# Row-shifted copies for three depthwise convolutions: sixteen on-chip transfers of 32 partitions in place of a DRAM round trip, and a shorter lag of one convolution

## The reference, cut to what matters

```python
t = t + dwconv(t, cpe1_w, cpe1_b)             # "cpe1"
tn = layernorm(t)
act_res = silu(tn @ actproj_w + actproj_b)
ti = silu(dwconv(tn @ inproj_w + inproj_b, dwc_w, dwc_b))      # "dwc"
out = linear_attention(ti) + dwconv(ti, lepe_w, lepe_b)        # "lepe"
t = shortcut + (out * act_res) @ outproj_w + outproj_b
```

## Time and profile before

| what | value |
|---|---|
| median of the runs shown (lowest, highest) | 3899.55 us (3897.82, 3903.65) |
| the profiled execution's own time | 3894.08 us |
| its span, first to last instruction | 3892.3 us |
| PE busy | 2998.4 us, 77% |
| DVE busy | 2489.5 us, 64% |
| ACT busy | 2366.1 us, 61% |
| POOL busy | 1088.2 us, 28% |
| mean granted TensorE clock | 0.92 of full speed |
| loads of shifted rows | 3 x 192 transfers of 196 KB, 3.8 to 3.9 us from issue to landing |
| stores to the scratch tensors | 3 x 48 transfers of 392 or 490 KB |

### The profile page before, as it was taken

One profiled execution on the slowest core, in us unless ns is written; L12 is line 12 of the kernel. 1 busy time (PEld: TensorE's weight loads), 2 busy tenths in 40 slices (PEclk: granted clock), 3 DMA queues, 4 the chain that ended last, 5 costly groups with the idle time before them and its releaser, 6 DMA issues. The chain is left out here.

```text
span 3892.3 us, 53786 instructions
## 1 busy us (share of the span) xinstructions
PE 2998.4 (77%) x17500; PEld 1615.2 (41%) x17500; DVE 2489.5 (64%) x2565; ACT 2366.1 (61%) x2681; POOL 1088.2 (28%) x612
## 2 busy tenths in 40 slices
PE   3678766969968876697996877677898778768699
PEld 2344334435534432543553433343454334344355
DVE  5677546876568644787466964578735886466871
ACT  3788434458778743546777864443767876444485
POOL 0235002632034500363103530046210452014530
PEclk9899988989989998898998999888999999988899
DMA  2001454600200146350020024644002004455201
GB/s 67 12 1 33 117 136 147 164 9 0 74 17 0 38 118 191 107 144 9 0 90 1 0 74 110 188 119 107 9 9 81 0 0 112 110 167 143 67 0 49
DMA packets 137194, 274.36 MB, mean 70 GB/s; under 512 B 17139, under 2 KB 93622, under 8 KB 137014
## 3 DMA queue, kind: packets, MB, share of 16 engines
q1 hardware_dynamic: 137014, 272.01, 25.3%
HBM read 194.07 MB, written 77.88 MB: 70 GB/s over the span
## 5 line engine op out<-in xcount | busy, mean ns | idle before, releaser
L1472 DVE SCALAR_TENSOR_TENSOR work<-region,cols,work 128x768 f32<-128x768 f32 x288 | 392.1, 1361 | 15.1 <-DVE work L1472 7.5
L664 POOL TENSOR_TENSOR region<-region 128x768 f32<-128x768 f32 x96 | 211.0, 2201 | 370.8 <-ACT region L844 365.1
L995 PE MATMUL psum<-region,m_fc 128*128 128x384 f32 (+1 forms) x768 | 282.2, 490 | 11.2 <-ACT work L946 11.2
L1241 PE MATMUL psum<-work,m_fc 128*128 128x384 f32 x768 | 282.6, 491 | 0.0
L995 PE MATMUL psum<-region,m_cen 128*128 128x384 f32 (+1 forms) x384 | 165.6, 557 | 136.5 <-DVE region L1585 62.3
L625 POOL TENSOR_TENSOR work<-work 128x768 f32<-128x768 f32 x48 | 113.9, 2377 | 501.8 <-ACT work L764 415.2
L1391 DVE SCALAR_TENSOR_TENSOR work<-region,cols,work 128x768 f32<-128x768 f32 x144 | 202.3, 1430 | 78.3 <-POOL work L625 62.3
L639 POOL TENSOR_TENSOR work<-work,region 128x768 f32<-128x768 f32 x96 | 174.3, 1816 | 235.0 <-DVE work L1406 235.0
L995 PE MATMUL psum<-work,m_avg 128*128 128x384 f32 x576 | 225.5, 516 | 15.6 <-ACT work L806 7.7
L217 DVE SCALAR_TENSOR_TENSOR region<-region,cols 128x768 f32<-128x768 f32 x192 | 223.8, 1166 | 16.7 <-POOL region L664 8.7
L678 POOL COPY region<-work 128x768 f32<-128x768 f32 x4 | 3.3, 823 | 818.6 <-DVE work L1509 818.6
(11 more groups left out here) (234 smaller groups left out, 7495.6 us busy)
## 6 DMA issues: line engine op xcount, KB each, us to landing
work<-scratch_cpe SPq DMA_DIRECT2D x192, 196.0 KB, 3.8
work<-scratch_dwc SPq DMA_DIRECT2D x192, 196.0 KB, 3.8
work<-scratch_lepe SPq DMA_DIRECT2D x192, 196.0 KB, 3.9
region<-in_tab_ch SPq DMA_DIRECT2D x48, 768.0 KB, 5.3
region<-in_x SPq DMA_DIRECT2D x48, 384.0 KB, 3.3
region<-in_tab_tok SPq DMA_DIRECT2D x48, 384.0 KB, 3.1
out<-work SPq DMA_DIRECT2D x48, 384.0 KB, 2.3
scratch_cpe<-region SPq DMA_DIRECT2D x44, 392.0 KB, 4.6
```

Of the source, the lines that this page charges most:

```text
L664: g.tensor_tensor(chain_tile(conv, n, p), chain_tile(conv, n - 1, p), chain_tile(conv, n, p), ALU.add).then_inc(tap_done[n], 1)
L995: last = pe.matmul(psum[:, bank + s, 0:HC], weights[:, :], moving(s), start=(n == 0), stop=(n == len(terms) - 1))
L1241: last = pe.matmul(psum[:, 4 + s, 0:HC], fc2[:, P * j:P * (j + 1)], static(tile(4 + j))(s), start=(j == 0), stop=(j == 3))
L1472: v.scalar_tensor_tensor(out=by_row(tile(acc + p)), in0=prow(k, b, *TAPS[n]), scalar=tap_weight(conv, TAPS[n]), in1=by_row(tile(acc + p)), ...
```

## The change

The DRAM tensors, the stores and the waits for them go. `fetch_shifted` now copies straight from the image in SBUF: for each channel group j and each q one transfer of 32 partitions x 1568 bytes (49 KB), so 16 per block. SP issues those of j = 0 and 1, ACT those of j = 2 and 3, eight each. ACT's eight stand in its own order of work: first in the step in cpe1 (lag 0), behind `silu_act` in dwc (lag 2), first in the step in lepe (lag 1). Each of the two waits, before it issues block b, for block b+1 of the image and for PE's convolution of block b-2. In the dwc stage the lags are shortened: PE and DVE take block t-3 and no longer t-6, ACT's `dwc_centre` t-2 (was t-5) and `silu_v` t-4 (was t-7).

```diff
-    scratch = {c: nc.dram_tensor("scratch_" + c, [P, SP * SP], F32).ap() for c in ("cpe1", "dwc", "lepe")}
...
+        def fetch_shifted(eng, groups, k, b, p, landed_sem):
+
+            for j in groups:
+                for q in range(4):
+                    eng.dma_start(shifted_rows(p)[32 * q:32 * q + 32, GROUP * j:GROUP * (j + 1)],
+                                  R[k][32 * j:32 * j + 32, ds(ROWS * SP * b + 2 * SP * q, GROUP)]).then_inc(landed_sem, 16)
...
-                def fetch_shifted(conv, b, p, landed_sem):
-
-                    for q in range(4):
-                        rows = scratch[conv][:, ds(ROWS * SP * b + 2 * SP * q, GROUP)]
-                        sp.dma_start(shifted_rows(p)[32 * q:32 * q + 32, :].rearrange("c (j x) -> c j x", j=4),
-                                     rows.rearrange("(j c) x -> c j x", j=4)).then_inc(landed_sem, 16)
...
                 def load_x_shifted(b, p):
-                    rows_landed(x_stored, b, p)
+                    sp.wait_ge(d_out, done(i, following(b)))
+                    sp.sem_inc(rows_seen, 1)
                     sp.wait_ge(e1["conv"], done(i, b - 2))
-                    fetch_shifted("cpe1", b, p, x_shifted[p])
...
+                    fetch_shifted(sp, (0, 1), 0, b, p, x_shifted[p])
...
-                pipelined(sp, NB, [(2, load_x_shifted), (0, store_x)])
-                pipelined(sp, NB, [(2, load_ti_shifted), (0, store_ti)])
-                pipelined(sp, NB, [(0, store_v)])
+                pipelined(sp, NB, [(0, load_x_shifted)])
+                pipelined(sp, NB, [(0, load_ti_shifted)])
...
+                def load_x_upper(b, p):
+                    a.wait_ge(d_out, done(i, following(b)))
+                    a.sem_inc(halves_seen, 1)
+                    a.wait_ge(e1["conv"], done(i, b - 2))
+                    fetch_shifted(a, (2, 3), 0, b, p, x_shifted[p])
...
-                pipelined(a, NB, [(0, cpe1_centre), (3, squares), (4, root)])
+                pipelined(a, NB, [(0, load_x_upper), (0, cpe1_centre), (3, squares), (4, root)])
...
-                pipelined(a, NB, [(0, silu_act), (5, dwc_centre), (7, silu_v)])
+                a.wait_ge(e1["conv"], done(i, NB - 1))
+                pipelined(a, NB, [(0, silu_act), (2, load_ti_upper), (2, dwc_centre), (4, silu_v)])
...
+                def load_upper(b, p):
+                    a.wait_ge(f2_conv, done(i, b - 2))
+                    fetch_shifted(a, (2, 3), 0, b, p, v_shifted[p])
+
-                pipelined(a, NB, [(0, query_exp), (1, reciprocal), (1, lepe_centre)])
+                a.wait_ge(e2_conv, done(i, NB - 1))
+                pipelined(a, NB, [(1, load_upper), (0, query_exp), (1, reciprocal), (1, lepe_centre)])
...
-                pipelined(pe, NB, [(0, in_act), (6, dwc)])
+                pipelined(pe, NB, [(0, in_act), (3, dwc)])
...
-                pipelined(v, NB, [(6, left), (6, right), (0, ti), (6, add_taps)])
+                pipelined(v, NB, [(3, left), (3, right), (0, ti), (3, add_taps)])
```

More of the change, by code:

```diff
@@ L312, in build @@
         f2_tab = [sem(f"f2_tab{n}") for n in range(2)]
-        v_stored = sem("v_stored")
-        x_stored = [sem(f"x_stored{n}") for n in range(2)]
         x_shifted = [sem(f"x_shifted{n}") for n in range(2)]
-        ti_stored = [sem(f"ti_stored{n}") for n in range(2)]
         ti_shifted = [sem(f"ti_shifted{n}") for n in range(2)]
@@ L319, in build @@
         rows_seen = sem("rows_seen")
+        halves_seen = sem("halves_seen")
         side_taps = sem("side_taps")
@@ L518, in load_tok_table, with load_ti_shifted @@
                         .then_inc(f1_tab[p], 16)
-                def stored_rows(b):
-                    return ds(ROWS * SP * b, (ROWS + 2 if isinstance(b, int) and b == NB - 1 else ROWS) * SP)
-                def fetch_shifted(conv, b, p, landed_sem):
-                    for q in range(4):
-                        rows = scratch[conv][:, ds(ROWS * SP * b + 2 * SP * q, GROUP)]
-                        sp.dma_start(shifted_rows(p)[32 * q:32 * q + 32, :].rearrange("c (j x) -> c j x", j=4),
-                                     rows.rearrange("(j c) x -> c j x", j=4)).then_inc(landed_sem, 16)
[L530 to L541, removed]
                 def load_x_shifted(b, p):
-                    rows_landed(x_stored, b, p)
+                    sp.wait_ge(d_out, done(i, following(b)))
+                    sp.sem_inc(rows_seen, 1)
                     sp.wait_ge(e1["conv"], done(i, b - 2))
-                    fetch_shifted("cpe1", b, p, x_shifted[p])
-                def store_ti(b, p):
+                    fetch_shifted(sp, (0, 1), 0, b, p, x_shifted[p])
+                def load_ti_shifted(b, p):
                     if is_first(b):
@@ L551, in store_ti @@
                         sp.sem_inc(rows_seen, 1)
[L552 to L557, removed]
                         sp.wait_ge(e1["conv"], done(i, NB - 1))
                         sp.sem_inc(rows_seen, 1)
+                    sp.wait_ge(e2_ti, done(i, following(b)))
+                    sp.sem_inc(rows_seen, 1)
                     sp.wait_ge(e2_conv, done(i, b - 2))
[L561 to L565, removed]
+                    fetch_shifted(sp, (0, 1), 3, b, p, ti_shifted[p])
                 def load_shifted(b, p):
@@ L570, in load_shifted @@
                         sp.sem_inc(rows_seen, 1)
+                    sp.wait_ge(e2_v, done(i, following(b)))
+                    sp.sem_inc(rows_seen, 1)
                     sp.wait_ge(f2_conv, done(i, b - 2))
[L572 to L575, removed]
+                    fetch_shifted(sp, (0, 1), 0, b, p, v_shifted[p])
                 def load_ch_table(b, p):
@@ L881, in dwc_centre, with load_ti_upper @@
                                  bias=col("dwc_b")).then_inc(e2_centre, 1)
+                def load_ti_upper(b, p):
+                    a.wait_ge(e2_ti, done(i, following(b)))
+                    a.sem_inc(halves_seen, 1)
+                    a.wait_ge(e2_conv, done(i, b - 2))
+                    fetch_shifted(a, (2, 3), 3, b, p, ti_shifted[p])
                 a.wait_ge(borders, i * 5 + 4)
-                pipelined(a, NB, [(0, silu_act), (5, dwc_centre), (7, silu_v)])
+                a.wait_ge(e1["conv"], done(i, NB - 1))
+                pipelined(a, NB, [(0, silu_act), (2, load_ti_upper), (2, dwc_centre), (4, silu_v)])
                 def stage(b, p):
@@ L1126, in dwc @@
                 def dwc(b, p):
-                    pe.wait_ge(ti_shifted[p], i * (32 * NB) + (b * 32 + (64 - 32 * p)))
+                    pe.wait_ge(ti_shifted[p], i * (128 * NB) + (b * 128 + (256 - 128 * p)))
                     pe.wait_ge(e2_sum, done(i, b - 2))
```

4 lines of the change are left out of this document (2 added, 2 removed).

## The result

The changed kernel takes **4082.1 us** (4080.2 to 4087.3, four runs); the kernel before, beside it, 3898.7 us. The ratio is 1.047 (95% interval 1.046 to 1.049): slower by 4.7%. Forecast were 3858 us and a range of 3770 to 3965, so sign and range were both missed.

What follows compares the result with a forecast made beforehand. SP's round of store landed, four loads, next store (7.05 us a block) was taken to bound cpe1 and dwc, PE lepe. -1.5 - 16 + 7 = -10.5 per image, x 4 = -42 us, gave 3858 us, range 3770 to 3965.

Steps and rivals of the forecast that it cites:

- What bounds the kernel now: In cpe1 and dwc SP's round of store landed, four loads, next store, 7.05 us a block; in lepe PE, 8.75.
- The price of one issue: On each queue, all three stages: 0.49 us between issues, eight taking 3.9 us a block, bounds 2.7 and 5.1.
- Landing: From the last issue to landing of the new transfers: 2.7 us, with a bound above of some 4.1.
- Rival 3: Slow landing, 4.1 us after the last issue, or copies crowd: -3 us per image, 3888 us; chance 0.12.
- 0.85 us hidden beside one ACTIVATE: On ACT: its sequencer goes on once an instruction has begun, so issuing hides about 0.85 us of one ACTIVATE.
- rival 4: ACT's sequencer does not go ahead with a DMA, 0.85 us not hidden: +2.5 per image, 3910 us; chance 0.10.
- cpe1, -1.5 forecast: In cpe1 SP's round goes and ACT's step becomes 6.45 us against 7.05: -1.5 us per image.
- not late: In cpe1 PE does not hold up the step, its own being 2.2 + 1.5 + 1.5 = 5.2 us.
- dwc, -16 forecast: In dwc no SP round, a drain three blocks shorter, a two-step loop of 11.7 us (5.85 a step): -16 us per image.
- lepe, +7 forecast: In lepe ACT's issues delay the exponentials and what waits on them, 9.45 us a block against 8.75: +7 us per image.
- Rival 1: The two queues exclude each other, or ACT's issue is dearer than SP's: L 5.1 us everywhere, 3972 us; chance 0.22.
- L: Time of eight issues per block on each queue, SP and ACT: 3.9 us, bounds 2.7 and 5.1.

Runs made afterwards that it cites:

- c1: The kernel before, with SP's loads in cpe1 and dwc issued one step later, DRAM route kept: 3787.3 us, ratio 0.971.
- e1: The kernel before, each block read back from DRAM by sixteen small transfers on SP instead of four large ones: 4208.3 us, ratio 1.080.
- e2: The kernel before, stores kept, its four large loads per block reading the chip's own memory instead of DRAM: 3927.3 us, ratio 1.008.
- e10: The changed kernel, with ACT's eight transfers per block reading the input in DRAM instead of the tensor on the chip: 4000.9 us, ratio 1.026.
- e8: The changed kernel, with ACT's exponentials in lepe run ahead of its eight transfers: 3995.7 us, ratio 1.024 to the kernel before.
- e5: The changed kernel with the old lags of dwc put back (6, 5, 7 for 3, 2, 4): 4106.9 us, ratio 1.052 to the kernel before.
- e3: The changed kernel with ACT's eight transfers left out, its waits and SP's eight kept: 3806.6 us, ratio 0.977 to the kernel before.
- e7: The changed kernel, with ACT's root (Ln and Exp) in cpe1 run ahead of its eight transfers: 4157.0 us, ratio 1.067 to the kernel before.

## Why the prediction was wrong, point by point

- **What bounds the kernel now: right.** c1 takes away SP's waits for its stores and keeps everything else of the DRAM route, and gains 2.9%.
- **The price of one issue: the step that failed first.** I took 0.49 us between issues (bounds 0.34 and 0.64), from rows whose source is DRAM, while the copies of the change have both ends on the chip. Here one issue lasts 0.53 to 0.57 us, and eight take 5.1 to 5.5 us in most blocks (5.4 on average), not 3.9: at or above the upper bound of 5.1. e1, e2 and e10 show that source and not shape makes the difference. The bound above, 0.64, came from one pair of the setup, and is about where ACT's pitch lies: (5.07 - 0.53)/7 = 0.65.
- **Landing: wrong side, harmless.** 1.9 us instead of 2.7; not because the DRAM read is gone (e1's small transfers from DRAM land in 1.8, e2's large ones from the chip in 3.7), but because the transfers are the small ones. Rival 3 is out. The rule of "DMA: Bandwidth & Descriptors" of the Trainium skill, section "Rules for kernel authors", that many small transfers should be joined, is borne out by e1 (sixteen for four cost 311 us). What is paid there is the issue of each one, 0.51 us from one to the next, and not a slower landing; and in the change it is paid on an engine that also computes.
- **0.85 us hidden beside one ACTIVATE: right in mechanism, wrong in size, both ways.** ACT's sequencer does go ahead with a DMA (e8: the issues begin at 767.40, 0.2 us after L905 began; rival 4 is out). It goes further than I read from the earlier trace rows: in dwc an issue begins before two ACTIVATEs ahead of it have begun, and more than 0.85 us is hidden. But in cpe1 the convolution awaited ends only when ACT is almost through. In image 0, from the sixth block on, the issues begin between 0.6 us before the end of the last ACTIVATE and 0.8 us after it, on average with it. To this cover I gave 0.85 us in every step; there it was worth nothing.
- **cpe1, -1.5 forecast, +27.3 measured.** The stage lies 28.8 us above its forecast. Most of that is in the seven steps that I put at 6.45 each, 45.2 us in all: from load 4 (426.50) to load 11 (491.95) they took 65.4, 9.35 a step. Of the 20.3 us more, the longer issues make 12.5 (5.7 us a block with the long ones, not 3.9), the cover that isn't there 6.1, and the hop after the last issue, which I left out, 1.8. I had also called PE "not late" by its own work alone, 5.2 us. That isn't its lateness: the convolution stands behind centre and variance, which wait through DVE for ACT's Exp. And as PE idles for it, its granted clock over the stage falls from 0.97 to 0.86, and centre and variance last up to 2.9 and 2.8 us instead of 1.5 each (457.45 and 460.15 in the trace, after 5.88 us of idle). Stage windows, before and after (busy time by engine, then the clock, DMA share, GB/s):

```profile
386.87:489.97 103.10, 74.49 (x705) 34.79 (x703) 54.05 (x61) 49.34 (x58) 8.06 (x12) 0.97 0.44 111
```

```profile
391.04:521.40 130.36, 85.35 (x705) 37.37 (x703) 53.64 (x61) 48.96 (x57) 7.98 (x12) 0.86 0.28 68
```

  ACT computes for 49 us in both; what is added is time in which it issues or waits.
- **dwc, -16 forecast, -5.4 measured.** Sign right, and the loop of two steps is the one I named. From issue start 556.79 to 570.43 it is 13.6 us, not 11.7: issues 5.5 (3.9), landing 1.6 (2.7), convolution 2.2, 1.0 until DVE has given ti, `in_act` 2.8, and 0.5 to the next issue. The 1.0 and the 0.5 are not in my sum. (My text names `silu_act` in this loop and my sum leaves its 0.9 us out; in the trace the issue begins before `silu_act` does, at 570.43 against 570.76.) From issue start 556.79 to 597.21 a step is 6.7 us on average, not 5.85. The shorter drain is worth some 6 us an image (e5), and the clock over the stage rose, from 0.83 to 0.92.
- **lepe, +7 forecast, +24.1 measured.** The chain was named rightly and is in the trace link by link: issues, exponentials, `weigh`, `turned`, `attend`, `convolve`. Its sum of 18.9 us for two blocks became 21.3 at the fast clock: issues with their hops 5.9 instead of 4.5, and `weigh` and `turned` 5.8 instead of 4.9, mostly since POOL's second product lasted 2.52 us there where the earlier trace rows have 1.82 (its median over all blocks is 2.17 us after, 1.81 before; why it is slower was not tested). In the pair at 743.23 PE ran at a granted clock of 0.69 from `attend` on, the pair took 24.1, and the 2.8 us more are all PE's. That term is nowhere in the prediction, and it is larger than the other two together (2.3 us). I took the order of ACT's step as given and never asked what it cost; e8 shows that it was nearly all of lepe's loss.
- **The rivals.** Rival 1 came nearest: slower, because ACT's issue is dearer. Its first half is out: SP's issues last 0.527 to 0.528 us alone (e3) and beside ACT's. The Trainium skill, page "Perfetto Trace Analysis", section "DMA Instruction — HWDGE (DVE, Sync)", has the generator locked for one issuer at a time; no run here shows such a lock in the length of the typical issue. The few long ones (up to 2.1 us) are not it, for they come with SP issuing alone too (up to 1.9 us in e3); the 96 issues of SP of 0.6 to 0.9 us may be. And its 3972 us, at L = 5.1, is 110 us short, because the slopes start from a step that already left out ACT's lost cover, the hop and PE's clock.
- **The range.** It was built on the bounds of one number, L. Two more were unknown, how much of L hides and what ACT's order exposes. Both could cost far more than they could give, and neither was in the range.

## What to carry to other kernels

Before moving DMA issues to an engine that computes, price one issue from a row with the same source and the same destination, and count it as that engine's work: here eight issues (5.1 to 5.5 us) outweighed ACT's four ACTIVATEs (3.4 us), and the eight transfers cost 275 of 4082 us. If they must be there, try their place in the step: behind what other engines wait for (e8, 86 us better), and where they hide another engine's reply (e7, which gave that up, was 75 us worse). And where a queue waits for its own store, first try to ask for the data one step later: that alone, with the trip through DRAM kept, won 2.9%.

## What the hardware did that I had not expected

- An issue of a row copy from the chip to the chip lasts 0.527 us (49 KB) to 0.610 us (196 KB) on SP; the same copy out of DRAM 0.316 us for either size, and a store from the chip to DRAM 0.375. On ACT from the chip the median is 0.569, from DRAM 0.466 with a minimum of 0.317.
- The landing of these row copies doesn't go by the source: 1.8 to 2.0 us for 49 KB and 3.7 to 3.9 us for 196 KB, from either (4.0 and 4.2 in c1). Size alone doesn't set it: an image block of 384 KB lands in 3.3 us.
- ACT's sequencer issues a DMA before ACTIVATEs ahead of it in the program have begun (563.31 against 563.51 and 564.24 us), if no wait holds it.
- An idle of 3.24 us of PE in lepe was followed once by a stretch at a granted clock of 0.69 (8.93 us of work) and once by one at 1.00 (6.16 us for the same work).
- Two queues that issue at the same time don't lengthen each other's typical issue (0.528 us on SP either way). A few issues last 1.0 to 2.1 us: 37 of 2304 in the changed kernel, 14 of them beside a long one of the other queue, and 23 of 1152 with SP alone (e3). What they are is open.
